# Moving the end of one head's weighted sum behind the next head's third score tile, in a two-layer gated cross-attention kernel

## The chip, the cores and the metric

The kernel runs on one core of one Trainium2 chip. The metric is the device time of one execution in microseconds (us), lower is better. Engines are named as in the profile: PE does matmuls, DVE is the vector engine, ACT the scalar engine, POOL the general one, and SP only issues DMAs here.

## The reference

Four stages, each added to x with a tanh gate: cross-attention (layer 0), a top-1 routed FFN, a second cross-attention, and a top-2 routed FFN. The change is in the first alone:

```python
xn = _layernorm(x, gamma_media, beta_media)        # media: ctx, 8 x 512 x 256
ln = _layernorm(latents, gamma_lat, beta_lat)      # latents: layernorm(x)
q = ln @ Wq + bq                                   # 8 heads of 128
kv = concatenate([xn, ln], axis=1) @ Wkv + bkv     # 1024 keys
attn = softmax(einsum('bhid,bhjd->bhij', q * DH ** -0.5, k))
out = einsum('bhij,bhjd->bhid', attn, v)
return out.reshape(b, -1, INNER) @ Wo + bo
```

There are 8 batches (b) with 8 heads each, 512 queries and 1024 keys: 64 heads in all.

## The kernel before, in words

**Tiling.** A head (n = 8 b + 2 hp + par, with hp from 0 to 3 and par 0 or 1) is one pass of `step(b, hp, par)` on each engine. Its scores are four tiles of 128 queries by 1024 keys, in two slots of PSUM (`ps_s`, tile qt in slot qt % 2). Everything else PE makes goes through a ring of four PSUM banks (`pj`): use u of the ring may begin when use u - 4 has been read out (`free_bank`, semaphore `pj_out`). Each product is three matmuls, of high and low halves (`mm3`), so each result is read out twice: ACT writes the high half (`use_bank` of ACT), DVE then the low half (`use_bank` of DVE, semaphore `hi_done`).

**The order of the work** is a string per kind of head in `plan` (L176). Every engine walks through it in that order and takes what concerns it. The words are:

- `scores0` to `scores3`: PE makes a score tile, DVE its row maximum (L605), ACT its exponential into `prob` (L489, `exp`). `scores2` waits on PE for the exponential of tile 0, `scores3` for that of tile 1.
- `qk0`, `qk1`, `qk2`: the query projection and the two halves of the key projection for the next head, six matmuls of 512 columns each. ACT L466, DVE L543.
- `v0` to `v3`: value projections for the next two heads, only where par is 0. ACT L468, DVE L542.
- `tr0`, `tr1`: DVE turns tiles 0 and 1 of `prob` in blocks of 32 by 32 (L600, `turn_blocks`). PE and ACT skip these words.
- `hi0`, `hi1`: ACT makes the high half of a turned tile (L481, `staged_high`), POOL then its low half (L414, `low`).
- `turn2`, `turn3` (each `left` and `right`): tiles 2 and 3 are turned on PE through the ring instead (L819). ACT L471, DVE L542. Tile 3 is turned in the next head.
- `fin0`, `fin1`: twice twelve matmuls of 512 columns, the weighted sum of the head that ends, n - 1, in one bank. It is read out after `fin1` (ACT L477, DVE L542). `fin0` waits for tile 3 turned and for both low halves of POOL.
- `out0`, `out1`: the output projection of that head, added to `x_acc` by DVE (L574). `out0` waits for the read-out of `fin1` on DVE.
- `zt`, `lg`, `cn`: small matmuls of the routing of the batch before. `pro`: transposes of the next batch's input. `tb`: a product for the bias, once, in head 0 (L827).

**Between tr and hi** stands a round trip to memory, in `step` of SP: `write_blocks(n, 0)`, `write_blocks(n, 1)` (L299), `regroup(n, 0)`, `regroup(n, 1)` (L305, four DMAs each), in this order. SP's queue is in order: the regroup of tile 0 is issued behind the write of tile 1, and that write waits for `tr1` on DVE.

**Other work of DVE** hangs on words of the plan: some of it is done right after `tr0`, some right after the row maximum of `scores2`. In head (hp, par) of a batch it is: (0,0) `init_acc` after `tr0`; (0,1) `route_measure` after `tr0`, `route_normalise` after `scores2` (in batch 0 `init_acc`, and L729 after `scores2`); (1,0) `statistics` parts 0 and 1; (1,1) part 2 after `tr0`; (2,0) `route_relate`, then `route_number` and `route_choose`; (3,0) `route_add_up` (L1193), then `route_number_rows`. Those named route are there from batch 1 on.

**ACT** keeps one exponential back: a score tile that is followed by something other than `fin` or another score tile (the `tr` words left out) has its exponential behind the next read-out of the plan (`late`, L506). Otherwise the exponential comes at once.

Of the kernel before, what the change touches and what calls it, by code (L numbers as in the profile page):

```python
# [43 lines left out]
def flat(ap):  # L44

    n = len(ap.shape) - 1
    names = "abcd"[:n]
    return ap.rearrange(f"p {' '.join(names)} -> p ({' '.join(names)})") if n > 1 else ap
# [11 lines left out]
def layer0_attention(nc, t_in, K, tg, route, x1_dram, tables, qk_dram, blocks_dram):  # L60
# [11 lines left out]
    with ExitStack() as ctx:  # L72
# [103 lines left out]
        def plan(b, hp, par):  # L176

            n = 8 * b + 2 * hp + par
            if par == 0:
                steps = "scores0 turn3 qk0 qk1 scores1 tr0 fin0 tr1 scores2 fin1 scores3 qk2 v0 hi0 v1 v2 hi1 out0 turn2 v3 out1"
            elif hp == 1 and b:
                steps = "scores0 turn3 qk0 zt0 zt1 scores1 tr0 fin0 tr1 scores2 fin1 scores3 lg0 qk1 qk2 hi0 out0 turn2 hi1 out1"
            elif hp == 2 and b:
                steps = "scores0 turn3 qk0 scores1 tr0 fin0 tr1 scores2 fin1 cn0 scores3 qk1 qk2 hi0 out0 turn2 hi1 out1"
            elif hp < 3:
                steps = "scores0 turn3 qk0 scores1 tr0 fin0 tr1 scores2 fin1 scores3 qk1 qk2 hi0 out0 turn2 hi1 out1"
            elif b < B - 1:  # L190
                steps = "scores0 turn3 pro2 scores1 pro3 scores2 pro0 tr0 fin0 tr1 scores3 fin1 qk0 pro1 qk2 out0 hi0 qk1 turn2 hi1 out1"
            else:
                steps = "scores0 turn3 scores1 tr0 fin0 tr1 scores2 fin1 scores3 hi0 out0 turn2 hi1 out1"
            for qt in "23":
                steps = steps.replace("turn" + qt, "left" + qt + " right" + qt)
            steps = [(step[:-1], int(step[-1])) for step in steps.split()]
            if n == 0:
                steps = [step for step in steps if step[0] not in ("fin", "out") and step not in (("left", 3), ("right", 3))]
                steps.insert(steps.index(("qk", 2)) + 1, ("tb", 0))
            return steps  # L200

        def is_use(step):
            return step[0] in TURNS + ("qk", "v", "out", "pro", "zt", "lg", "cn", "tb") or step == ("fin", 1)
# [7 lines left out]
        for n in range(B * H0):  # L211
            uses = [step for step in plan(n // 8, n % 8 // 2, n % 2) if is_use(step)]
            if ("qk", 2) in uses:
                KEYS_DONE[n + 1] = START[n] + max(uses.index(("qk", 1)), uses.index(("qk", 2))) + 1
            for j in range(1, 4, 2):
                if ("pro", j) in uses:
                    LAID[n, j // 2] = START[n] + uses.index(("pro", j)) + 1
            for qt in range(2, TB):
                if ("right", qt) in uses:
                    TURNED[n - (qt == 3), qt] = START[n] + uses.index(("right", qt)) + 1  # L220
            for use in (("zt", 1), ("lg", 0), ("cn", 0)):
                if use in uses:
                    ROUTED[use, n // 8 - 1] = START[n] + uses.index(use) + 1
            if n:
                FIN_DONE[n - 1] = START[n] + uses.index(("fin", 1)) + 1
                OUT_DONE[n - 1] = START[n] + uses.index(("out", 1)) + 1
            START.append(START[n] + len(uses))
            HIGH_START.append(HIGH_START[n] + sum(highs(use) for use in uses))
# [215 lines left out]
        def _(act):  # L444
# [10 lines left out]
            def use_bank(use, u, bank, n, par, b):  # L455

                kind, j = use
                src = pj[:, bank, :]
                if not highs(use):
                    return  # L460
                if use == ("qk", 0) and n < 0:
                    act.wait_ge(set_up, 2)
                act.wait_ge(pj_full, u + 1)
                if kind == "qk":
                    i = min(j, 1)
                    a(qk_dst(0, j, 1 - par), src, ACT.Identity, bias=bias[:, (n + 1) % H0, i:i + 1]).then_inc(hi_done, 1)  # L466
                elif kind == "v":
                    a(flat(v[0][:, 2 * j:2 * j + 2, :]), src, ACT.Copy).then_inc(hi_done, 1)  # L468
                elif kind in TURNS:
                    half = TURNS.index(kind)  # L470
                    a(pT[0][:, 4 * half:4 * half + 4, j * P:(j + 1) * P], src.rearrange("p (k q) -> p k q", k=4), ACT.Copy).then_inc(hi_done, 1)  # L471
                elif kind == "pro":

                    c, half = j % 2, j // 2
                    a(kvT[0][:, c, half * S:(half + 1) * S], src, ACT.Copy).then_inc(hi_done, 1)
                else:
                    a(oT[0][:], src, ACT.Copy).then_inc(hi_done, 1)  # L477

            def staged_high(n, t):
                act.wait_ge(turned_back[t], 64 * n + 64)  # L480
                a(by_query(pT[0], t), from_blocks(staged[t]), ACT.Copy).then_inc(turned_hi, 1)  # L481

            def exp(n, qt, par):
                act.wait_ge(max_done, 4 * n + qt + 1)
                if n and qt >= 2:
                    act.wait_ge(pj_full, TURNED[n - 1, qt])
                elif n and qt == 1:
                    act.wait_ge(turned_lo, TILES * (n - 1) + qt + 1)
                a(prob[:, qt, :], ps_s[:, qt % 2, :], ACT.Exp, bias=neg_max[:, qt:qt + 1],  # L489
                  accum_out=row_sum[:, par, qt:qt + 1]).then_inc(exp_done, 1)  # L490
# [8 lines left out]
            def step(b, hp, par):  # L499
                n = 8 * b + 2 * hp + par  # L500
                u = START[n]
                late = None
                steps = [at for at in plan(b, hp, par) if at[0] != "tr"]
                for (kind, j), following in zip(steps, steps[1:] + [None]):

                    if kind == "scores" and following[0] not in ("fin", "scores"):  # L506
                        late = j
                        continue
                    if kind == "scores":
                        exp(n, j, par)  # L510
                    elif kind == "hi":
                        staged_high(n, j)
                    elif is_use((kind, j)):
                        use_bank((kind, j), u, u % RING, n, par, b + 1)
                        u += 1
                    if late is not None and kind != "left":
                        exp(n, late, par)
                        late = None
                    if n == 1 and (kind, j) == ("scores", 1):
                        act.wait_ge(big_hi, 1)  # L520
                        act.wait_ge(wo_load, 16)
                        a(flat(wo[0][:]), wo_in, ACT.Identity, scale=tg[:, 0:1]).then_inc(big_hi, 1)
                    if b and (hp, par) == (2, 0) and (kind, j) == ("right", 2):
                        route_exponentials(route, act, b - 1)

            def pair(b, hp):
                step(b, hp, 0)
                step(b, hp, 1)
# [7 lines left out]
        def _(dve):  # L536
# [147 lines left out]
            def step(b, hp, par):  # L684
# [4 lines left out]
                ahead = b < B - 1  # L689
                late = None  # L690
                for kind, j in plan(b, hp, par):
                    if kind == "hi":
                        continue
# [552 lines left out]
def route_exponentials(r, act, b):  # L1246
    act.wait_ge(r.step, route_done(r, "rel", b))
    r.nc.scalar.activation(flat(r.ex[:]), flat(r.rel[:]), ACT.Exp).then_inc(r.exp_done, 1)
# [1676 lines left out]
```

## Time and profile before

| | |
|---|---|
| time, median of 3 runs | 3000.14 us (2997.01 to 3000.71) |
| the profiled execution | 3000.29 us |
| its span, first to last instruction | 2998.7 us |
| layer 0 attention with its weights | from about 31 us to 1472 us of the span |
| PE in stretch 400 to 600 us | busy 198.05 of 200 us, granted clock 1.00 |
| DVE, ACT, POOL in the same stretch | 161.59, 110.57 and 97.06 us busy |

All times inside the kernel are microseconds from the start of the span. The profile gives each matmul an end that is modelled; neighbouring matmuls overlap in it, so PE's pace is read from start to start. A wait is told by the engine, its line, and the work that ended last before it.

### The profile page before, as it was taken

What the parts mean: (1) busy time and instruction counts of PE and PEld (TensorE: products, weight loads), DVE (VectorE), ACT (ScalarE), POOL (GpSimd) and SP (SyncE); (2) the same over time, 40 slices, a digit from 0 to 9 for tenths busy, and PEclk for the clock granted to TensorE, in tenths of its full rate; (3) what the DMA queues carried; (4) which work ended last, traced back from release to release, by engine and by line L of the source; (5) the groups of instructions that cost most, each with busy time, mean ns of one, the idle gap of its engine ahead of it and who ended that gap; (6) DMA issues with size and microseconds to landing.
All of it is one profiled execution on the core that took longest, in us unless ns stands there. A gap on an engine that the chain in (4) does not pass through costs nothing. (4 is left out here: it accounts for less than half of the span.)

```text
span 2998.7 us, 46707 instructions
## 1 busy us (share of the span) xinstructions
PE 2824.4 (94%) x17032; PEld 2283.2 (76%) x17032; DVE 2203.2 (73%) x3482; ACT 1789.4 (60%) x2774; POOL 1706.1 (57%) x1054
## 2 busy tenths in 40 slices
PE   6999999999999999999599779999999967999999
PEld 5888888888888888888599644555555437999999
DVE  6778877888878788877545567777777535588887
ACT  4565555555555555555355348888888833466665
POOL 4544545454454454442334338888887724478886
PEclk9999999999999999999799879999999988999999
DMA  5764353443534434443356354444333023278885
GB/s 173 214 200 116 109 141 97 119 131 100 140 105 131 116 106 123 110 118 102 115 199 226 114 170 120 120 121 115 113 105 107 23 85 133 98 214 234 225 231 147
DMA packets 295880, 409.73 MB, mean 137 GB/s; under 512 B 30323, under 2 KB 216850, under 8 KB 295664
## 3 DMA queue, kind: packets, MB, share of 16 engines
q1 hardware_dynamic: 274864, 375.28, 41.8%
q0 software_dynamic: 18656, 29.00, 4.9%
q8 instruction: 129, 2.11, 0.3%
q10 hardware_dynamic: 2144, 2.62, 0.3%
q14 instruction: 87, 0.71, 0.1%
HBM read 259.51 MB, written 149.04 MB: 136 GB/s over the span
## 5 line engine op out<-in xcount | busy, mean ns | idle before, releaser
L1774 POOL TENSOR_TENSOR c_pT_lo<-c_prob,c_pT_hi 128x1024 fp32r<-128x1024 f32 x192 | 456.3, 2383 | 115.6 <-ACT c_pT_hi L1857 111.3
L489 ACT ACTIVATE a_prob<-a_scores,a_neg_max 128x1024 f32<-128x1024 f32 x256 | 286.0, 1117 | 384.8 <-DVE a_neg_max L605 384.5
L414 POOL TENSOR_TENSOR a_pT_lo<-a_turned,a_pT_hi 128x1024 fp32r<-128x1024 f32 x64 | 153.3, 2395 | 612.1 <-ACT a_pT_hi L481 612.1
L1969 DVE TENSOR_REDUCE c_neg_max<-c_max 128x2 f32<-128x1024 f32 x248 | 302.1, 1218 | 72.6 <-PE c_max L2202 71.4
L605 DVE TENSOR_REDUCE a_neg_max<-a_scores 128x1 f32<-128x1024 f32 x256 | 308.8, 1206 | 10.7 <-PE a_scores L36 9.9
L1851 ACT ACTIVATE c_prob<-c_scores 128x1024 f32<-128x1024 f32 x256 | 261.2, 1020 | 72.9 <-PE c_scores L2213 68.5
L34 PE MATMUL m_h<-m_rT_hi,m_w_hi 128*128 128x256 f32 x880 | 253.7, 288 | 1.9 <-DVE m_rT_lo L2703 1.9
L35 PE MATMUL m_h<-m_rT_lo,m_w_hi 128*128 128x256 f32 x880 | 248.7, 283 | 0.0
L36 PE MATMUL m_h<-m_rT_hi,m_w_lo 128*128 128x256 f32 x880 | 248.5, 282 | 0.0
L2598 POOL TENSOR_TENSOR m_w_lo<-m_w_in,m_w_hi 128x1024 fp32r<-128x1024 f32 x80 | 199.6, 2494 | 61.7 <-ACT m_w_hi L2646 60.6
L1857 ACT ACTIVATE c_pT_hi<-c_prob 128x1024 fp32r<-128x1024 f32 x192 | 203.5, 1060 | 13.7
L34 PE MATMUL a_scores<-a_kT_hi,a_qT_hi 128*128 128x512 f32 x512 | 205.0, 400 | 3.0 <-DVE a_kT_lo L543 1.6
L34 PE MATMUL a_pj<-a_pT_hi,a_v_hi 128*128 128x512 f32 x512 | 204.2, 399 | 1.7 <-DVE a_pT_lo L542 1.7
L36 PE MATMUL a_pj<-a_pT_hi,a_v_lo 128*128 128x512 f32 x512 | 204.4, 399 | 0.0
L35 PE MATMUL a_pj<-a_pT_lo,a_v_hi 128*128 128x512 f32 x512 | 203.1, 397 | 0.0
L35 PE MATMUL a_scores<-a_kT_lo,a_qT_hi 128*128 128x512 f32 x512 | 201.4, 393 | 0.0
L36 PE MATMUL a_scores<-a_kT_hi,a_qT_lo 128*128 128x512 f32 x512 | 200.2, 391 | 0.0
L2703 DVE TENSOR_TENSOR m_hT_lo<-m_g,m_hT_hi 128x256 fp32r<-128x256 f32 x220 | 186.9, 850 | 13.2 <-ACT m_hT_hi L2668 7.6
L471 ACT ACTIVATE a_pT_hi<-a_pj 128x512 fp32r<-128x512 f32 x256 | 138.8, 597 | 91.0 <-PE a_pj L819 91.0
L34 PEld LDWEIGHTS m_h<-m_rT_hi,m_w_hi 128*128 128x128 f32 x880 | 166.4, 189 | 2.3 <-DVE m_rT_lo L2703 2.3
L35 PEld LDWEIGHTS m_h<-m_rT_lo,m_w_hi 128*128 128x128 f32 x880 | 167.1, 190 | 0.0
L36 PEld LDWEIGHTS m_h<-m_rT_hi,m_w_lo 128*128 128x128 f32 x880 | 166.6, 189 | 0.0
(353 smaller groups left out, 9018.7 us busy)
## 6 DMA issues: line engine op xcount, KB each, us to landing
m_w_in<-L_ffn_w_in SPq DMA_DIRECT2D x117, 512.0 KB, 5.3
blocks_dram<-a_turned SPq DMA_DIRECT2D x64, 512.0 KB, 2.6
blocks_dram<-a_prob SPq DMA_DIRECT2D x64, 512.0 KB, 2.9
a_turned<-blocks_dram SPq DMA_DIRECT2D x256, 128.0 KB, 3.3
a_prob<-blocks_dram SPq DMA_DIRECT2D x256, 128.0 KB, 3.6
e_w_in<-L_ffn_w_in SPq DMA_DIRECT2D x32, 1024.0 KB, 6.7
qk_dram<-c_stage SPq DMA_DIRECT2D x64, 256.0 KB, 3.5
c_q_rows<-qk_dram SPq DMA_DIRECT2D x32, 512.0 KB, 5.0
```

Source lines behind the costliest of these rows:

```text
L34: pe.matmul(out, l_hi, r_hi, start=start, stop=False)
L35: pe.matmul(out, l_hi, r_lo, start=False, stop=False)
L36: return pe.matmul(out, l_lo, r_hi, start=False, stop=stop)
L414: g.tensor_tensor(by_query(pT[1], t), from_blocks(staged[t]), by_query(pT[0], t).bitcast(F32), ALU.subtract).then_inc(turned_lo, 1)
L489: a(prob[:, qt, :], ps_s[:, qt % 2, :], ACT.Exp, bias=neg_max[:, qt:qt + 1], accum_out=row_sum[:, par, qt:qt + 1]).then_inc(exp_done, 1)
L605: ve.tensor_reduce(neg_max[:, qt:qt + 1], ps_s[:, qt % 2, :], AX.X, ALU.max, negate=True).then_inc(max_done, 1)
L1774: g.tensor_tensor(flat(pT[1][:, kt - 1]), flat(prob[:, kt]), flat(pT[0][:, kt - 1]).bitcast(F32), ALU.subtract).then_inc(lo_pool, 1)
L1851: a(flat(prob[:, kt]), flat(ps_s[:]), ACT.Exp).then_inc(exp_done, 1)
L1857: a(flat(pT[0][:, kt - 1]), flat(prob[:, kt]), ACT.Copy).then_inc(hi_act, 1)
L1969: ve.tensor_reduce(two, max_bank(n, qt)[:], AX.X, ALU.max, negate=True).then_inc(max_done, 1)
L2598: nc.gpsimd.tensor_tensor(w[1][:, m % 2, j], w_in[:, m % 2, j], w[0][:, m % 2, j].bitcast(F32), ALU.subtract).then_inc(w_lo, 1)
L2703: return ve.tensor_tensor(out, value, hi.bitcast(F32), ALU.subtract)
```

## The change

The plans of the heads that have `fin0 tr1` behind the second score tile are reordered. One key projection moves from behind `scores3` to behind `scores1`, the two halves of the weighted sum move one score tile later, and `tr1` moves from ahead of `scores2` to behind it. The plan of (3,1) and that of the last head stay. In ACT, the exponentials of tiles 1 and 2 now also come at once where `qk` or `lg` follows.

```diff
@@ plan
             if par == 0:
-                steps = "scores0 turn3 qk0 qk1 scores1 tr0 fin0 tr1 scores2 fin1 scores3 qk2 v0 hi0 v1 v2 hi1 out0 turn2 v3 out1"
+                steps = "scores0 turn3 qk0 qk1 scores1 tr0 qk2 scores2 tr1 fin0 scores3 fin1 v0 hi0 v1 v2 hi1 out0 turn2 v3 out1"
             elif hp == 1 and b:
-                steps = "scores0 turn3 qk0 zt0 zt1 scores1 tr0 fin0 tr1 scores2 fin1 scores3 lg0 qk1 qk2 hi0 out0 turn2 hi1 out1"
+                steps = "scores0 turn3 qk0 zt0 zt1 scores1 tr0 qk1 scores2 lg0 tr1 fin0 scores3 fin1 qk2 hi0 out0 turn2 hi1 out1"
             elif hp == 2 and b:
-                steps = "scores0 turn3 qk0 scores1 tr0 fin0 tr1 scores2 fin1 cn0 scores3 qk1 qk2 hi0 out0 turn2 hi1 out1"
+                steps = "scores0 turn3 qk0 scores1 tr0 qk1 scores2 tr1 fin0 scores3 fin1 cn0 qk2 hi0 out0 turn2 hi1 out1"
             elif hp < 3:
-                steps = "scores0 turn3 qk0 scores1 tr0 fin0 tr1 scores2 fin1 scores3 qk1 qk2 hi0 out0 turn2 hi1 out1"
+                steps = "scores0 turn3 qk0 scores1 tr0 qk1 scores2 tr1 fin0 scores3 fin1 qk2 hi0 out0 turn2 hi1 out1"
@@ step of ACT
-                    if kind == "scores" and following[0] not in ("fin", "scores"):
+                    if kind == "scores" and following[0] not in ("fin", "scores") and not (following[0] in ("qk", "lg") and j in (1, 2)):
```

In head 0 the words `fin` and `out` are taken out and `tb` is put behind `qk2`; so `qk2 tb` now stands ahead of `scores2` there.

## Rows read from the trace of the kernel before

**Rows 1.** Windows: stretch, length, busy PE, PEld, DVE, ACT, POOL, granted clock, DMA

```profile
400.00:600.00 200.00, 198.05 (x1110) 169.54 (x1109) 161.59 (x267) 110.57 (x185) 97.06 (x65) 1.00 0.42 115
```

**Rows 2.** Waits of PE, 60 to 1475 us: total, times, longest

```profile
PE a_pj L819 <- DVE a_v_lo L542: 8.6, 12, 0.7
...
PE a_pj L34 <- DVE a_kT_lo L543: 4.4, 17, 0.3
```

**Rows 3.** Timeline, DVE in head (3,0) of batch 1: start, length, instruction

```profile
344.36 4.64 DVE L1193 TENSOR_TENSOR r_sums<-r_sums,r_counts 128x16 f32<-128x16 f32 x4
348.92 1.23 DVE L600 STREAM_TRANSPOSE a_prob<-a_prob 128x1024 f32<-128x1024 f32 x1
350.08 1.18 DVE L605 TENSOR_REDUCE a_neg_max<-a_scores 128x1 f32<-128x1024 f32 x1
```

**Rows 4.** POOL in the same head, and all instructions of L1193 (shortest, median, longest ns)

```profile
346.00 2.39 POOL L402 TENSOR_TENSOR a_y<-a_y,a_affine 128x1024 f32<-128x1024 f32 x1
...
L1193 DVE TENSOR_TENSOR r_sums<-r_sums,r_counts x32: 131/536/2299, 344.4 to 1488.4; 128x16 f32<-128x16 f32 x32
```

**Rows 5.** Timeline, SP's queue in the same head: write of tile 1, both regroups

```profile
350.18 0.34 SPq L299 DMA_DIRECT2D blocks_dram<-a_prob  x1
350.57 2.24 SPq L305 DMA_DIRECT2D a_turned<-blocks_dram  x4
353.16 1.74 SPq L305 DMA_DIRECT2D a_prob<-blocks_dram  x4
```

**Rows 6.** DMA issues: count, size, median us from issue to landing

```profile
a_turned<-blocks_dram SPq DMA_DIRECT2D x256, 128.0 KB, 3.3
a_prob<-blocks_dram SPq DMA_DIRECT2D x256, 128.0 KB, 3.6
```

**Rows 7.** Timeline, ACT in head (3,0) of batch 1

```profile
354.88 1.12 ACT L489 ACTIVATE a_prob<-a_scores,a_neg_max 128x1024 f32<-128x1024 f32 x1 [1.30 <-DVE a_neg_max L605]
...
356.46 1.05 ACT L481 ACTIVATE a_pT_hi<-a_turned 128x1024 fp32r<-128x1024 f32 x1
```

**Rows 8.** Timeline, PE at the end of the same head

```profile
356.33 0.28 PE L35 MATMUL a_pj<-a_wo_lo,a_oT_hi 128*128 128x256 f32 x1
356.45 0.28 PE L36 MATMUL a_pj<-a_wo_hi,a_oT_lo 128*128 128x256 f32 x1
357.44 0.63 PE L819 MATMUL a_pj<-k_ident,a_prob 128*128 128x128 f32 x4 [0.71 <-DVE a_v_lo L542]
```

**Rows 9.** Timeline, DVE in head (0,1) of batch 2, which begins at 406.4

```profile
415.87 1.25 DVE L600 STREAM_TRANSPOSE a_prob<-a_prob 128x1024 f32<-128x1024 f32 x1
...
418.15 1.36 DVE L1160 TENSOR_SCALAR z<-x_acc,r_mv,r_rstd 128x256 f32<-128x256 f32 x4
```

**Rows 10.** Timeline, DVE in head (1,0) of batch 2, first and last of six of `statistics`

```profile
437.87 0.41 DVE L631 BATCH_NORM_STATS2 a_stats<-a_x_in 128x6 f32<-128x256 f32 x1
...
439.11 0.17 DVE L633 BATCH_NORM_AGGREGATE a_mv<-a_stats 128x2 f32<-128x6 f32 x1
```

**Rows 11.** Timeline, DVE in head (2,0) of batch 2, which begins at 471.05

```profile
481.48 1.23 DVE L600 STREAM_TRANSPOSE a_prob<-a_prob 128x1024 f32<-128x1024 f32 x1
...
485.78 0.23 DVE L1186 TENSOR_TENSOR r_chosen<-k_iota,r_best 128x64 f32<-128x64 f32 x1
...
491.19 0.69 DVE L542 TENSOR_TENSOR a_v_lo<-a_pj,a_v_hi 128x512 fp32r<-128x512 f32 x1 [0.74 <-ACT a_v_hi L468]
```

**Rows 12.** Timeline, ACT in the same head

```profile
489.61 1.06 ACT L481 ACTIVATE a_pT_hi<-a_turned 128x1024 fp32r<-128x1024 f32 x1
```

**Rows 13.** Timeline, PE in head 0

```profile
39.65 0.50 PE L34 MATMUL a_scores<-a_kT_hi,a_qT_hi 128*128 128x512 f32 x1 [1.47 <-ACT a_prob L489]
...
41.15 0.40 PE L34 MATMUL a_pj<-a_kvT_hi,a_wqk_hi 128*128 128x512 f32 x1
...
42.54 3.61 PE L827 MATMUL a_pj<-a_y,a_bias 128*128 128x256 f32 x16
```

**Rows 14.** Timeline, PE at the end of the stage: from `fin1` to `out0` with nothing between

```profile
1469.79 0.35 PE L34 MATMUL a_pj<-a_wo_hi,a_oT_hi 128*128 128x256 f32 x1 [1.46 <-issue]
```

## The prediction

> **What bounds the kernel now.** First the windows: from 400 to 600 us PE is busy 198.05 of 200 us at granted clock 1.00, every other engine far less [rows 1]. The work of PE is the same after the change, so a reordering can only remove or add gaps of PE. Then PE's waits, 60 to 1475 us: two kinds recur, 12 waits for `a_v_lo` (8.6 us) and 17 for `a_kT_lo` (4.4 us) [rows 2]. The second is `out1` of heads (0,1) and (2,1), which waits for the ring bank of `qk2`; counted from start to start it costs about 0.4 us each, by the profile's idle 0.26. The first is head (3,0): `left2` starts 0.99 us after the last `out0` matmul instead of 0.12, and `right2` is late as much again [rows 8], 1.75 us a head, in six batches. So at most some 17 us of gaps recur. Last I read the queues beside PE, because the change moves `tr1`, and behind `tr1` hangs a chain.
>
> **The chain from tr1 to PE.** In head (3,0) `tr1` ends at 350.15 [rows 3]. SP issues the write of tile 1 at 350.18 and only behind it the regroup of tile 0 at 350.57, taking 2.24 us [rows 5]; the last of the four lands 3.3 us after its issue [rows 6]. So the data of `hi0` is there about 0.4 + 2.2 + 3.3 = 5.9 us after `tr1`, at 356.05, and ACT starts `hi0` at 356.46 [rows 7]: 0.4 us to spare. The regroup of tile 1 begins when its write has landed, 3.0 us after `tr1` [rows 5], and is there 3.0 + 1.7 + 3.6 = 8.3 us after `tr1` [rows 5, 6]. ACT goes in order: with `hi0` late, the read-out of `v1` is late, DVE's low half of it too, and `right2` on PE waits for that bank. In head (2,0) `tr1` ends at 482.71, so the data is there at 488.6, ACT starts `hi0` at 489.61 [rows 11, 12]: 1.0 to spare. The low half of `v1` ends at 491.88 [rows 11], PE wants `right2` at about 492.6: 0.6 more to spare. Whatever `tr1` is delayed by beyond 1.6 us is lost there.
>
> **What delays tr1.** On DVE it now stands behind the low half of a key tile (0.7, as the low half of `v1` [rows 11]), the row maximum of `scores2` (1.2 [rows 3]) and whatever hangs on `scores2`. I take batches 1 to 6, times from the head's start.
> - (0,0): 0.7 + 1.2 = 1.9, less small idle; just covered: 0.
> - (0,1): it began at 415.87, which is 9.45; ahead of it come the low half of `qk1` (0.7), a row maximum (1.2 less overlap) and `route_normalise` (1.36 [rows 9]): `tr1` starts at 12.6, and the row maximum of `scores3` ends near 15.0. Now `fin1` follows the exponential of tile 3 on ACT, where it had been followed by the score tile: exponential 1.1 [rows 7], high half 0.6, low half 0.7, so `out0` may start at 17.45; PE is there at 16.2. Lost: 1.25. `hi0` waits until 13.8 + 5.9 = 19.7; the low half of `left2` ends at 22, where PE wants the bank for `right3` of the next head at 21.5: 0.5 lost. ACT carries some lateness on. Sum 1.75.
> - (1,0): 0.7 + 1.2 and `statistics` part 1, from 437.87 to 439.28, 1.4 [rows 10]: delay 3.1, less 1.6, plus 0.4 carried from (0,1): 1.9.
> - (1,1): two small stages cover most; but `qk2` alone now stands between `fin1` and `out0`. The pair with nothing between, at the end of the stage, starts `out0` 1.46 us after the last record of `fin1` had ended [rows 14], 1.6 us after the next stage could have started. A stage of six matmuls is 42.54 - 41.15 = 1.4 us [rows 13]. Lost: 0.2.
> - (2,0): `route_choose` ends at 486.01 as before [rows 11] (it starts earlier, but see below), `tr1` then at 487.2 instead of 482.7: delay 4.45, less 1.6: 2.8.
> - (2,1): `cn0` covers `out0`; 0.
> - (3,0): `route_add_up` (4.64 us) stays ahead [rows 3]; `tr1` comes 0.7 + 1.2 + 0.7 to 1.0 later, say 3.0, with 0.4 to spare; PE already waits for this chain: 2.6 on top of the 1.75.
> - (3,1) keeps its plan: 0.
>
> Sum 1.75 + 1.9 + 0.2 + 2.8 + 2.6 = 9.25. Two waits for `qk2` of 0.42 go, since ACT no longer puts the exponential of tile 3 between `qk1` and `qk2`: 8.4 us a batch, 50.5 in six.
>
> Batch 7 has no statistics and little POOL work: 1.75 + 0.5 + 0.2 + 1.7 - 0.8 = 3.3. In batch 0, head 0 has `qk2 tb` ahead of `scores2`: this covers PE's wait of 1.47 [rows 13], but `tr1` is behind the read-out of `tb` (a row of 3.61 us on PE, some 3.3 to the next start [rows 13]) and moves from 40.9 to 47.0; `hi0`, at 48.6 before, comes near 53, `v1` is read out near 54.6, and `v3` waits for its bank: the head ends 3.6 later. Head (0,1) there has L729 and ACT's `a_wo_hi` ahead; its read-outs and then `out0` are some 4 late. With 2.5 for the next three: 10 us. Sum of all: 50.5 + 3.3 + 10 = 64 us. The profiled execution took 3000.29 (span 2998.7), 0.15 above the median, so 3064.
>
> **Edits that I cost at nothing.** The exponentials of tiles 1 and 2 come at once where `qk` or `lg` now follows; that keeps the old order of ACT, and the key's high half (0.7) waits behind one exponential; PE needs that bank four uses later, so it is covered. Without the edit `tr1` would come another 0.7 later. `fin0` one score tile and one key projection later only relaxes its wait for POOL. But the exponential of tile 1 also waits for POOL's second low half of the head before: with `hi1` at 8.3 after `tr1`, then 1.1 and 2.4 us, it is done some 5 us into the next head in the worst case, (0,1), and that exponential comes at 8. The weight loads on SP stand behind the regroups and come 2 to 4 us later; they are used two heads later. If either cover is gone, the loss is that of the third rival.
>
> Unknown is how much of a delay other engines absorb. Bounds for the delay of `tr1` in the plainest head: 1.2 (the row maximum alone, the key's low half fitting into idle time) and 1.9 plus 0.7 if DVE also waits for ACT's high half; that is -0.7 to +0.7 a head, on four heads a batch some 20 us either way. I take 1.9: DVE has no idle time there in the heads that lose [rows 3]. For gaps of PE and the clock: it was 1.00 in the stretch with gaps [rows 1]; I count no change.
>
> **The lock.** In (3,0) the four additions of L1193, of 16 elements, take 4.64 us, and single ones 131 to 2299 ns [rows 3, 4]; POOL's operation from 346.00 lasts 2.39, the time of the longest. So DVE stood still while POOL worked, and moved work of that kind ends when POOL ends: this is why I leave the end of `route_choose` in (2,0) where it was. The Trainium skill, "SBUF — State Buffer", section "Who interferes with whom", says a DVE instruction with two SBUF inputs waits for a POOL instruction that reads SBUF, whole; the trace agrees. By unblocked times (2,0) would lose 0.5 less, 3 us in all.
>
> **Rivals.**
> - *PE stays covered* (faster). For it: spare time of 1.0 and 0.6 in (2,0), ring banks taken earlier, 17 waits and the one in head 0 gone: -7.1 - 1.5 = -8.6, so 2992. Against: it needs `tr1` less than 1.6 late in (2,0), where 4.45 is expected, and (3,0) has 0.4. It decides if the regroup of tile 0 does not stand behind `tr1`; SP's order of issue says it does [rows 5]. A variant loses just as much as it gains: 3000.
> - *Only the routing heads lose*: (2,0) and (3,0) as above, all others covered, since DVE's idle time takes their delays in. 6 x (2.8 + 2.6 - 0.84) + 4 for head 0 = 31: 3031. For it: (0,1) and (1,0) rest on chains of small numbers that were worked out, not seen.
> - *The delay feeds itself*: `hi1` late makes the next head's first exponential, its `tr1` and so its `hi0` late; each loss of a batch carried on at half its size: 50.5 x 1.5 + 13 = 89, so 3089. Against: (3,1) and (2,1) have room and reset it.
>
> **How the numbers follow.** Chances: forecast 0.62, routing heads only 0.2, feeding itself 0.1, covered 0.05, no change 0.03. 0.2% (6 us) is about what a measurement can tell from no change. Faster 0.05, same 0.03, slower 0.92. The forecast's own spread is 20 us each way; the range takes in the routing case and most of the third: 3025 to 3088.
>
> **What would show it.** Right: ACT's L481 now waits for the DMA of `a_turned` in the heads with par 0; PE's waits for `a_v_lo` grow from 12 to over 20 and from 0.7 to 2 us or more; new waits of PE for `a_oT_lo` before `out0`, longest in (0,1); head (2,0) of batch 2 near 27 us instead of 24.2, (3,0) near 28.8 instead of 26.2; `a_kT_lo` before `out1` gone; scores1 to scores2 in head 0 without a wait. Wrong: PE still busy 198 of 200 us, or L481 never waiting; then the chain behind `tr1` was not what binds.

## The result

The changed kernel takes 3081.51 us (median of 4 runs, 3076.89 to 3089.76), the kernel before 2998.57 beside it. The ratio is 1.0278, with a 95% interval from 1.0265 to 1.0291. The forecast was 3064, with a range of 3025 to 3088: the sign and the mechanism of the waits held, and the loss was 83 us where 64 were forecast. A second cost, TensorE's clock, had been put at nothing.

The profiled execution of the changed kernel took 3089.76 us (span 3088.1). Layer 0 holds nearly all of the difference: the first matmul of the stage behind it starts at 1564.06 instead of 1477.25, 86.8 us later, where the whole span is 89.4 longer. A window of the changed kernel, with the columns of [rows 1]:

```profile
400.00:600.00 200.00, 190.15 (x1034) 161.29 (x1033) 151.87 (x250) 104.97 (x172) 88.31 (x59) 0.98 0.43 116
```

PE did 1034 matmuls in 200 us instead of 1110 [rows 1], and the granted clock is no longer 1.00. Its waits in layer 0, 60 to 1570 us, and those of ACT's `hi` read-outs (total, times, longest), to be set beside [rows 2]:

```profile
PE a_pj L819 <- DVE a_v_lo L542: 48.8, 20, 3.8
...
PE a_pj L34 <- issue: 12.6, 9, 3.0
...
PE a_pj L34 <- DVE a_oT_lo L542: 4.9, 6, 1.0
```

```profile
ACT a_pT_hi L481 <- DMA a_turned<-blocks_dram: 79.3, 42, 4.0
...
ACT a_pT_hi L481 <- DMA a_prob<-blocks_dram: 23.3, 45, 1.2
```

The wait for `a_v_lo` grew from 8.6 us in 12 to 48.8 in 20, the wait for `a_kT_lo` is gone from the list, and ACT now waits 42 times for the turned tile 0 to come back. In the kernel before that wait came once, of 1.6 us. The waits named `issue` are `out0` waiting for the read-out of `fin1`: eight of the nine are in (0,1), 1.1 to 1.4 us in batches 1 to 7 and 3.0 in batch 0, and the ninth stands at the end of the stage in both kernels [rows 14].

**One head, step by step.** Head (3,0) of batch 2 begins at 550.55 and takes 30.7 us (26.2 before). DVE, the counterpart of [rows 3]:

```profile
559.49 4.66 DVE L1193 TENSOR_TENSOR r_sums<-r_sums,r_counts 128x16 f32<-128x16 f32 x4
564.07 0.74 DVE L543 SCALAR_TENSOR_TENSOR a_kT_lo<-a_pj,a_bias,a_kT_hi 128x512 fp32r<-128x512 f32 x1
564.74 1.21 DVE L605 TENSOR_REDUCE a_neg_max<-a_scores 128x1 f32<-128x1024 f32 x1
565.87 0.82 DVE L1199 TENSOR_TENSOR r_place<-r_counts,r_sums 128x64 f32<-128x64 f32 x1
...
566.87 1.24 DVE L600 STREAM_TRANSPOSE a_prob<-a_prob 128x1024 f32<-128x1024 f32 x1
```

`tr1` stands behind the key's low half, the row maximum and L1199, and begins 2.8 us later than right behind L1193. SP, the counterpart of [rows 5], then ACT:

```profile
568.13 0.34 SPq L299 DMA_DIRECT2D blocks_dram<-a_prob  x1
568.52 2.23 SPq L305 DMA_DIRECT2D a_turned<-blocks_dram  x4
```

```profile
570.83 0.60 ACT L468 ACTIVATE a_v_hi<-a_pj 128x512 fp32r<-128x512 f32 x1
574.17 1.06 ACT L481 ACTIVATE a_pT_hi<-a_turned 128x1024 fp32r<-128x1024 f32 x1 [2.75 <-DMA a_turned<-blocks_dram]
575.13 1.06 ACT L468 ACTIVATE a_v_hi<-a_pj 128x512 fp32r<-128x512 f32 x2
```

`hi0` starts 6.1 us after `tr1` ended (5.9 forecast), and ACT stood still for 2.75 with `v1` ready behind it. PE:

```profile
571.81 0.35 PE L34 MATMUL a_pj<-a_wo_hi,a_oT_hi 128*128 128x256 f32 x1 [0.68 <-DVE a_oT_lo L542]
...
576.49 1.12 PE L819 MATMUL a_pj<-k_ident,a_prob 128*128 128x128 f32 x4 [3.29 <-DVE a_v_lo L542]
...
577.83 0.41 PE L36 MATMUL a_pj<-a_wv_hi,a_kvT_lo 128*128 128x256 f32 x1
578.05 0.41 PE L34 MATMUL a_pj<-a_wv_hi,a_kvT_hi 128*128 128x256 f32 x1
```

Here is what the forecast left out. The matmuls behind the wait start 0.22 us apart instead of the 0.12 of [rows 8]. The window from the end of the wait to the end of the head tells why. The same stretch of head (2,0), here in batches 2 and 3, shows that it doesn't always happen:

```profile
576.49:581.25 4.76, 4.76 (x23) 4.76 (x24) 3.12 (x6) 2.62 (x4) 3.54 (x2) 0.50 0.06 14
```

```profile
528.52:531.35 2.83, 2.83 (x23) 2.65 (x24) 2.38 (x5) 2.54 (x5) 2.58 (x2) 1.00 0.04 11
...
719.40:724.16 4.76, 4.76 (x22) 4.76 (x23) 3.12 (x6) 2.77 (x5) 3.56 (x2) 0.50 0.03 6
```

The granted clock (last column but two) is 0.50, 1.2 GHz of 2.4, after waits of 3.29 us (576.49) and 2.90 us (719.40), and 1.00 after one of 2.87 us (528.52). The same work takes 4.76 us at the low level and 2.83 at the high one.

### The profile page after: what moved, and what is told of

The parts are those of the page before. It is cut to its first block and busy times, and to the rows that moved or that the text cites. A ratio compares the mean times of both kernels' runs of the same rounds, so it can differ in the third digit from the quotient of the medians.

```text
span 3088.1 us, 46707 instructions
## 1 busy us (share of the span) xinstructions
PE 2862.4 (93%) x17032; PEld 2311.2 (75%) x17032; DVE 2201.3 (71%) x3482; ACT 1797.4 (58%) x2774; POOL 1707.4 (55%) x1054
## 5 line engine op out<-in xcount | busy, mean ns | idle before, releaser
L819 PE MATMUL a_pj<-k_ident,a_prob 128*128 128x128 f32 x1024 | 144.3, 281 | 52.4 <-DVE a_v_lo L542 48.8
L542 DVE TENSOR_TENSOR a_pT_lo<-a_pj,a_pT_hi 128x512 fp32r<-128x512 f32 x256 | 164.1, 683 | 23.8 <-ACT a_pT_hi L471 23.7
L819 PEld LDWEIGHTS a_pj<-k_ident,a_prob 128*128 128x128 f32 x1024 | 120.8, 144 | 68.6 <-DVE a_v_lo L542 53.5
```

The lines of the kernel that those rows point to most:

```text
L819: last = t.transpose(dst[:, k * P:(k + 1) * P], prob[:, j, kt * P:(kt + 1) * P], ident[:])
```

## The experiments

Head lengths below are taken from the first score matmul of a head to that of the next, and averaged over batches 1 to 6. The medians come from four sessions, in which the kernel before took 2998.57 to 3001.36 us; each ratio further down is to the kernel before of the same session.

| kernel | (0,1) | (1,0) | (2,0) | (2,1) | (3,0) | (3,1) | median us |
|---|---|---|---|---|---|---|---|
| before | 19.04 | 24.24 | 24.23 | 19.47 | 26.18 | 20.42 | 2998.57 |
| changed | 19.92 | 26.69 | 28.06 | 19.32 | 30.51 | 20.68 | 3081.51 |
| e1, tr1 early | 19.89 | 24.22 | 24.67 | 19.22 | 25.62 | 20.48 | 3003.82 |
| e2, tr1 late alone | 19.04 | 26.44 | 28.38 | 19.47 | 29.60 | 20.49 | 3073.50 |
| e3, regroup first | 20.46 | 24.22 | 24.42 | 19.51 | 24.86 | 21.57 | 3021.83 |
| e4, extras behind | 19.90 | 24.27 | 24.68 | 19.21 | 28.38 | 20.51 | 3034.20 |
| e9, PE kept busy | 20.29 | 26.71 | 27.33 | 19.21 | 28.11 | 20.66 | 3069.37 |
| e6, add_up late | 19.02 | 24.25 | 24.24 | 19.47 | 24.24 | 20.40 | 2988.41 |

**e1: the new order, tr1 back behind tr0** (in all four plans).

```diff
-"... scores1 tr0 qk2 scores2 tr1 fin0 scores3 fin1 v0 ..."
+"... scores1 tr0 tr1 qk2 scores2 fin0 scores3 fin1 v0 ..."
```

> The changed kernel, but tr1 stands directly behind tr0 again (ahead of qk and scores2), in all four plans. Theory (the loss comes through tr1: its round trip through memory, then hi0 on ACT, the low half of v1, right2 on PE): nearly all of the loss is gone. Heads (1,0) and (2,0) of batch 2 are back at 24.2 to 24.5 us (26.6 and 27.4 in the changed kernel), (3,0) at 26 or a little less. (0,1) stays near 19.9, since its row maxima and the exponential of tile 3 still stand ahead of the read-out of fin1. Time 2990 to 3012 us. Rival (the loss comes from fin and qk: the read-outs of fin1 come too late for the ring and out0): the time stays above 3050 us. Third theory (the ACT order, exponentials ahead of the key's high half): also above 3050.

Measured 3003.82 us, ratio to before 1.0008 (0.9998 to 1.0017). The loss is gone, with `fin` and the key projections left where the change put them. (0,1) keeps its 0.85.

```profile
PE a_pj L819 <- DVE a_v_lo L542: 4.8, 6, 1.0
```

**e2: the order before, only tr1 behind scores2.**

```diff
-"... scores1 tr0 fin0 tr1 scores2 fin1 scores3 qk2 ..."
+"... scores1 tr0 fin0 scores2 tr1 fin1 scores3 qk2 ..."
```

> The kernel before, with one part of the change alone: tr1 moves behind scores2, fin0, fin1 and the key projections stay (tr0 fin0 scores2 tr1 fin1 scores3), and ACT is as before. Theory of tr1: delays by the row maximum 1.2 us, with the work that hangs on scores2 on top, 1.6 us of it covered: (2,0) loses 2.8 to 3.8 us a batch, (3,0) about 2, (1,0) about 1, (0,1) about 1.5: 7 to 8 us a batch, and 3035 to 3055 us in all. Rival (fin and qk make the loss): 2996 to 3006 us.

Measured 3073.50 us, ratio 1.0242 (1.0225 to 1.0259). The one word makes nearly all of the loss. It lies 18 us above the expectation, which was still worked out at full clock. In the profiled execution PE was busy for 41 us at granted clock 0.50 before the last head; by an estimate of half of that, some 20 us went there. The single terms were also off: (0,1) lost nothing where 1.5 were expected, (1,0) 2.2 for 1.

**e3: tile 0 comes back without waiting for tr1.**

```diff
                 write_blocks(n, 0)
-                write_blocks(n, 1)
                 regroup(n, 0)
+                write_blocks(n, 1)
                 regroup(n, 1)
```

> The changed kernel, but SP issues the regroup of tile 0 ahead of the write of tile 1, so tile 0 comes back without waiting for tr1. Theory of the chain: hi0 is in time everywhere, ACT's wait for a_turned (69 us in 35 waits, 200 to 1480 us) vanishes, PE's waits for a_v_lo fall from 48.8 to under 15 us. Left are hi1, still 8.3 us behind tr1, which costs up to 1 us in (2,0) and 2.5 in (3,0), the 1.3 of (0,1), and head 0: 3020 to 3045 us. Rival (the DVE order itself is the bound, by late read-outs): no more than 10 us better than the changed kernel.

Measured 3021.83 us, ratio 1.0073 (1.0056 to 1.0090). ACT's waits move from tile 0 to tile 1, and PE's for `a_v_lo` nearly go:

```profile
ACT a_pT_hi L481 <- DMA a_prob<-blocks_dram: 85.3, 57, 3.3
ACT a_pT_hi L481 <- DMA a_turned<-blocks_dram: 1.4, 1, 1.4
```

```profile
PE a_pj L819 <- DVE a_v_lo L542: 1.9, 6, 0.4
```

So three quarters of the loss went through the order of SP's queue. What is left sits in (0,1), (3,1) and batch 0. `hi1` is still late, but PE loses little by it: (3,0), where up to 2.5 us of loss were expected, is 1.3 shorter than in the kernel before.

**e4: the hanging work of DVE behind tr1.**

```diff
-                    elif after == ("scores", 2):
+                    elif after == ("tr", 1):
```

> The changed kernel, but the work of DVE that hangs on scores2 (route_normalise, statistics part 1, route_number and route_choose, route_number_rows, L729) is done behind tr1. Theory: tr1 is late only by the key's low half and the row maximum, about 1.9 us, of which 1.6 are covered in heads with par 0: (1,0) and (2,0) of batch 2 come to 24.3 to 24.8 us, (3,0) still loses about 2 us against before, (0,1) stays near 19.9: 3020 to 3040 us. Rival (the key's low half and the row maximum are the loss, the hanging work is not): above 3060 us.

Measured 3034.20 us, ratio 1.0116 (1.0097 to 1.0135). (1,0) is back, (2,0) to within 0.45 us, and (3,0) still loses 2.2 as expected: its long operation stands ahead of `tr1` in either order, and it has no room for the 1.9 us of key and row maximum.

**e5: 20 extra transposes ahead of right2 in (2,0) and (3,0).**

```diff
+                if use == ("right", 2) and b > 1 and hp in (2, 3) and n % 2 == 0:
+                    for _ in range(20):
+                        t.transpose(ps_s[:, 0, 0:P], ident[:], ident[:])
                 if use != ("fin", 1):
                     free_bank(u)
```

> The changed kernel, with 20 extra transposes of the identity on PE ahead of the wait of right2, in heads (2,0) and (3,0) of batches 1 to 7 (written to the free score slot, read by nobody). They add work of 2.2 us a head, inside a wait of 2.9 to 3.8 us. Theory of the clock: of the 83 us some 31 are not waits but matmuls at half pace after the long waits (granted clock 0.50 from 576.49 to 581.25 in the changed kernel); with PE kept busy the clock stays up in these heads and about 20 us come back: 3055 to 3070 us, and (3,0) falls from 30.7 to about 28.8 us. Rival (the waits are the whole loss, the slow matmuls come from memory or contention): no gain, 3078 to 3095 us.

Inconclusive in the time: 3080.15 us (3075.51 to 3083.68), ratio 1.0270 (1.0255 to 1.0286). The median missed the expectation by 10 us. In the profile (3,0) fell from 30.5 to 28.4 us, but the transposes cost 3.7 us in batch 7, where the wait was shorter than they are, and two heads (1,0) fell to the low clock that had not before. No run of the changed kernel stood beside it; e8 of the same session, that kernel but for ACT's edit, took 3086.78. So the test was repeated, sized to the waits and beside the changed kernel.

**e9 and e10: the transposes sized to the waits, beside the changed kernel.**

```diff
+                fill = 0
+                if use == ("right", 2) and n % 2 == 0 and 1 <= hp and b < 8:
+                    fill = {1: 30 if b == 1 else 10, 2: 0 if b == 1 else 24, 3: 0 if b == 1 else 28}[hp]
+                for _ in range(fill):
+                    t.transpose(ps_s[:, 0, 0:P], ident[:], ident[:])
```

and 24 more ahead of `out0` in head 1. (`b` is the batch plus one here.)

> The changed kernel with the extra transposes of PE sized to the waits: ahead of right2, 10 in (1,0), 24 in (2,0) and 28 in (3,0) of batches 1 to 6, 30 in (1,0) of batch 0, and 24 ahead of out0 in head (0,1) of batch 0 (2.6 to 3.3 us each where the wait is 3 us or more). Beside the changed kernel on the same chip (next run). Theory of the clock: 15 to 28 us less than the changed kernel, and no stretch of layer 0 between 60 and 1500 us at granted clock 0.50. Rival (waits alone): no difference beyond 5 us.

> The changed kernel as it is, on the chip of these runs, as the reference of e9: 3077 to 3090 us. If the clock's falls are what differs from run to run, its runs spread by 5 us or more where the kernel before spreads by 3.

Measured 3069.37 us with the transposes (ratio 1.0234, 1.0220 to 1.0248) and 3086.72 without (1.0291, 1.0277 to 1.0305). With 426 more matmuls on the busiest engine the kernel is 17 us faster. The queues are as late as before (ACT waits 80.7 us in 44 for tile 0), so what came back is the clock: between 60 and 1500 us thirteen stretches at 0.50 begin in e10 and one in e9. The expectation had none: this one, from 1012.1 to 1015.6, follows a wait of 1.92 us before `out0` of (0,1) in batch 5. Head (3,0) of batch 2, whole, and the stretch 400 to 600, in e9; then the same stretch in e10:

```profile
542.13:569.40 27.27, 27.27 (x172) 24.19 (x171) 19.63 (x30) 13.82 (x24) 18.97 (x11) 1.00 0.38 96
400.00:600.00 200.00, 197.52 (x1120) 168.62 (x1119) 153.56 (x250) 109.30 (x179) 97.48 (x66) 1.00 0.41 110
```

```profile
400.00:600.00 200.00, 190.72 (x1043) 162.06 (x1042) 152.51 (x253) 107.44 (x176) 90.73 (x60) 0.98 0.43 116
```

e10's runs spread by 8 us, those of e9 by 4. The first four runs of the changed kernel, 3089.76, 3085.63, 3077.39 and 3076.89 us, had mean granted clocks of 0.962, 0.963, 0.968 and 0.966: the slower ones were granted less, as they would be if the falls of the clock made the spread. That nothing else made it is not shown.

**e6: route_add_up and route_number_rows of (3,0) behind scores3**, in the kernel before.

```diff
-                        elif at == (3, 0) and b:            # behind tr0
-                            dve.wait_ge(pj_out, ROUTED[("cn", 0), b - 1])
-                            route_add_up(route, dve, b - 1)
...
-                        elif at == (3, 0) and b:            # behind scores2
-                            route_number_rows(route, dve, b - 1)
                     elif after == ("scores", 3):
+                        if at == (3, 0) and b:
+                            dve.wait_ge(pj_out, ROUTED[("cn", 0), b - 1])
+                            route_add_up(route, dve, b - 1)
+                            route_number_rows(route, dve, b - 1)
```

> The kernel before, but in head (3,0) route_add_up and route_number_rows of DVE are done behind the row maximum of scores3, when POOL has no long work. Theory of the lock: the five small operations take under 1.5 us there instead of 5.2, the waits of PE for v0 and v1 in (3,0) go (1.95 us a head, six heads): 2986 to 2992 us, ratio 0.996. Rival (L1193 is slow by itself): the head loses as much in its new place, 2998 to 3004 us.

Measured 2988.41 us, ratio 0.9958 (0.9945 to 0.9972). The four additions take 0.80 us in their new place instead of 4.64 [rows 3] (the line number is one less there, and POOL has nothing to do from 529.17 to 532.84):

```profile
529.28 0.80 DVE L1192 TENSOR_TENSOR r_sums<-r_sums,r_counts 128x16 f32<-128x16 f32 x4
```

**e7: the parts that gained, together.** e6, and e1's order in head 0 and in heads (2,1) of batches 1 to 7 only, with ACT's edit.

```diff
+            if n == 0:
+                steps = "scores0 turn3 qk0 qk1 scores1 tr0 tr1 qk2 scores2 fin0 scores3 fin1 v0 hi0 v1 v2 hi1 out0 turn2 v3 out1"
             elif hp == 2 and b:
+                steps = "scores0 turn3 qk0 scores1 tr0 tr1 qk1 scores2 fin0 scores3 fin1 cn0 qk2 hi0 out0 turn2 hi1 out1"
```

> The kernel before with the parts that gained: e6 (route_add_up late), and the new order with tr1 left behind tr0 in head 0 and in heads (2,1) of batches 1 to 7 only, with ACT's edit for them. Theory: on top of e6, about 1 us in head 0 and 0.26 us in seven heads (20.54 for 21.49 and 19.21 for 19.47 us with tr1 early): 2983 to 2990 us. Rival (head 0's new order sets back heads (0,1) and (1,0) of batch 0, which lost 3.2 and 0.3 us with tr1 early): no better than e6, 2988 to 2993.

Measured 2987.37 us, ratio 0.9955 (0.9941 to 0.9968). By time it can't be told from e6. By head, (2,1) gained the 0.26 us and head 0 one microsecond, of which the next two heads gave back 0.6.

**e8: ACT's edit taken back from head 2 on.**

```diff
-... and not (following[0] in ("qk", "lg") and j in (1, 2)):
+... and not (following[0] in ("qk", "lg") and j in (1, 2) and n < 2):
```

> The changed kernel with ACT's edit taken back from head 2 on: the exponential of tile 1 (and of tile 2 ahead of lg) again stands behind the next read-out. The prediction said tr1 would come another 0.7 us later: then 3090 to 3105 us. Rival, by the trace after: tr1 stands behind the row maximum of scores2 and the exponential of tile 1 has long ended by then, so it does not bind: 3072 to 3088 us, like the changed kernel.

Measured 3086.78 us, ratio 1.0290 (1.0275 to 1.0306), like e10's 3086.72 of a later session. The rival holds: no worth of the edit can be measured here.

**e11: e7 with the exponential of tile 3 behind both key projections.**

```diff
-                    if late is not None and kind != "left":
+                    if late is not None and kind != "left" and not (late == 3 and (kind, j) == ("qk", 1)):
```

> e7 (the best so far) with ACT's exponential of tile 3 behind the high halves of both key projections in heads (0,1), in place of between them. Theory: out1 no longer waits for the low half of qk2 there, 0.4 us in eight heads: 2981 to 2986 us. Rival: the exponential comes later, so hi0 and the next head's turn3 wait as long: 2985 to 2990 us, no difference from e7.

Measured 2983.36 us (2982.36 to 2985.89), ratio 0.9944 (0.9931 to 0.9958): the best of all, though its interval overlaps that of e7. PE no longer waits for `a_kT_lo` before `out1`, and (0,1) takes 18.76 us instead of 19.05; (1,0) gives back 0.2.

## Why the prediction was right, and where its size was off

- **The chain from tr1** was right in each link: L481 waits for the DMA (42 waits), `v1`'s low half follows it, and `right2` waits. e1 and e2 show that the word `tr1` makes nearly all of the loss, e3 that three quarters of it go through SP's order.
- **The signs that it named** came: no wait for `a_kT_lo` before `out1`, none between the score tiles 1 and 2 of head 0, and new waits before `out0`, longest in (0,1). The waits for `a_v_lo` came to 20, not over 20. Head (2,0) of batch 2 took 27.4 us for "near 27", (3,0) 30.7 for "near 28.8".
- **The terms**, net a batch over batches 1 to 6:

| head | forecast | measured |
|---|---|---|
| (0,0) | 0 | 0.06 |
| (0,1), less the wait for `qk2` gone | 1.75 - 0.42 = 1.3 | 0.9 |
| (1,0) | 1.9 | 2.45 |
| (1,1) | 0.2 | 0.1 |
| (2,0) | 2.8 | 3.8 |
| (2,1) | -0.42 | -0.15 |
| (3,0) | 2.6 | 4.3 |
| (3,1) | 0 | 0.26 |
| sum | 8.4 | 11.8 |

 Six batches gave 70.5 us for 50.5. Batch 7 gave 1.6 for 3.3, batch 0 gave 16.5 for 10. The rest is small: the last head and the end of the stage gave back about 3, and head 0 of the profiled execution began 1.25 later.
- **The step that failed** is "I count no change" for the clock. It rested on a stretch whose waits were at most 0.7 us [rows 2], while the forecast itself put waits of over 3 us in (3,0) and in batch 0. The trace of the kernel before had a row that spoke for such waits: in the last head of layer 0 PE waited 5.71 us, and from 1456.58 to 1465.00 its granted clock was 0.50.

```profile
PE a_pj L819 <- DVE x_acc L574: 5.7, 1, 5.7
...
1456.58:1465.00 8.42, 6.96 (x20) 5.57 (x21) 3.19 (x7) 1.20 (x2) 3.20 (x4) 0.50 0.14 49
```

 In the changed kernel, after the 3.29 us wait of (3,0), the four transposes, `v3` and `out1` took 4.76 us; in (2,0) of batch 2 they took 2.83 at full clock. That is 1.9 of the 4.3 us of (3,0), whose clock fell in all six batches. Without it the head lost 2.4, where 2.6 was forecast. (2,0) shows it from batch to batch: it lost 3.2, 3.2 and 2.8 us in batches 1, 2 and 4, where the clock stayed up, and 5.1, 4.5 and 4.1 in batches 3, 5 and 6, where it fell; 2.8 was forecast. The Trainium skill, "TensorE: Matmul & The Clock Gate", section "HAM oscillation — how this bites in real kernels", tells of a matmul loop whose clock falls behind each wait for data. The trace agrees for the six waits of (3,0), and only for three of six in (2,0).
- **A term that was too small** without the clock: in (1,0) it stayed up in all six batches, and the head lost 2.45 for 1.9. There `tr1` ended 4.1 us later than before (15.6 us into the head for 11.46), not 3.1 with 0.4 carried; 4.1 less the 1.6 of room is what was lost. In (2,0) and (3,0) `tr1` came 4.4 to 4.8 and 2.8 to 3.1 us later, close to the 4.45 and 3.0 of the forecast.
- **Counted over layer 0** of the profiled execution, matmul by matmul against the median pace of their kind: starts that came late behind an idle time sum to 84.7 us (29.2 before), starts at slowed pace to 44.3 (13.2 before). So of the 87 us, about 55 were waits and 31 pace; what counts as pace depends on the median taken, by some 8 us. A second estimate comes from the clock alone: ahead of the last head PE was busy for 60 us at granted clock 0.50, in twelve stretches (none before), and half of that is 30 us. The 64 of the forecast were all waits.
- **Luck**: the range reached 3088 for a spread of 20 us in the waits and for the rival in which the delay feeds itself. Neither was what filled it: the waits came out below the forecast and the clock made up for more than that. That 3081.5 lies inside the range is luck in this part, and the profiled execution, at 3089.76, lies outside.
- **Batch 0**: head 0 lost 3.7 us (3.6 forecast). (0,1) and (1,0) lost 5.9 and 6.6, where some 4 and, for (1,0) with the two heads behind it, 2.5 were forecast. `out0` of (0,1) waited 3.00 us and its matmuls then started 0.21 apart; (1,0) ran its last 4.75 us at 0.50:

```profile
108.50:113.25 4.75, 4.75 (x22) 4.75 (x23) 3.02 (x6) 2.41 (x4) 3.52 (x2) 0.50 1.00 319
```

- **Wrong without consequence**: that without ACT's edit `tr1` would come 0.7 later. By then `tr1` waits for DVE's own queue, not for the exponential (e8).
- **The lock**: that `route_choose` would end with POOL's work held. In (2,0) of batch 2 it ended at 518.84, 14.9 us into the head, as before. e6 turned the same reading into a gain.
- **The rivals**: with e1, where `tr1` is not delayed, the new order neither gains nor loses, so the gain of "covered" was not to be had by it. The delay does not feed itself: (3,1) takes 0.26 more than before. The routing heads alone would have left (1,0) and (0,1) as they were.

## What to carry to other kernels

Before a word is moved in one engine's order, list what each queue has behind it: here one operation of 1.2 us on DVE released a write, a read-back queued behind that write, and a read-out of ACT with others behind it, and the room was 1.6 us in (2,0) and 0.4 in (3,0). Where a forecast puts a new wait of two or three us on PE, price the clock as well: here one more fall of the clock cost 1.9 us behind a wait of 3.3, and a few matmuls that nobody reads, put into the wait, brought it back. Small vector operations beside long POOL work are worth moving: e6 got 12 us (3000.06 to 2988.41) from moving six of them in one head of each batch from batch 1 on.

## What had not been expected of the hardware

The length of the wait alone does not tell whether the clock falls. In head (2,0) of the changed kernel, with the same work around the wait, it stayed up behind a wait of 2.90 us in batch 1 (337.95) and fell behind one of 2.48 us in batch 6 (1292.11):

```profile
337.95:341.00 3.05, 3.05 (x24) 2.83 (x24) 2.00 (x4) 2.16 (x5) 2.19 (x2) 1.00 0.03 6
1292.11:1295.20 3.09, 3.09 (x15) 3.09 (x16) 2.71 (x5) 2.18 (x4) 2.98 (x2) 0.50 0.02 6
```

In the other runs it fell behind waits as short as 1.87 us (e10, 667.76) and stayed up behind 3.02 us (e4, 76.23). What else decides is not shown. So the time of a kernel with such waits can move with the number of falls: the changed kernel spread over 13 us in its first 4 runs, the kernel before over 4. And adding work to the bounding engine made a kernel faster: 3086.72 us to 3069.37.
